# A state-space stage with its convolution, point-wise and input matrices folded on chip into three shifted matrices, and one slot per sequence

## The reference

```python
rms = sqrt(mean(T * T, axis=-1) + 1e-6)
Tn = T / rms * norm_scale                      # T: 16 x 256 x 256
x, z = split(Tn @ in_w.T + in_b, 2)            # in_w: 512 x 256
gate = sigmoid(z)
xc = conv1d(x, dw_w, padding=1, groups=256) + dw_b     # 3 taps, each feature by itself
xc = pw_w @ xc + pw_b                          # over the features
y = ssm(xc, forward) + flip(ssm(flip(xc), backward))
#   ssm: u = x @ win.T (64 states); h = h * Abar + u * Bbar, step by step; (h * C) @ wout.T
y = (y * gate) @ out_w.T + out_b
out = T + y
...
x = layernorm(x + out)                         # so 2 * x + y, normalized over the features
```

## Time and profile before

| | |
|---|---|
| median of three runs | 2217.35 us (2207.57, 2219.92, 2217.35) |
| profiled execution | 2220.97 us, its span 2219.1 us |
| busy in the span | PE 1861.8 (84%), DVE 1285.6 (58%), ACT 1025.6 (46%), POOL 338.1 (15%) |
| mean granted TensorE clock | 0.916 |

### The profile page before, as it was taken

The page is one execution under the profiler, slowest core; times in us unless marked ns, Lnnn a source line. Parts: engine busy times, 40 slices in busy tenths (PEclk is TensorE's granted clock), DMA queues, the critical chain, the costliest instruction groups (busy, mean ns, idle before and its releaser), DMA issues. The chain is left out here.

```text
span 2219.1 us, 39960 instructions
## 1 busy us (share of the span) xinstructions
PE 1861.8 (84%) x14981; PEld 1647.3 (74%) x15076; DVE 1285.6 (58%) x2769; ACT 1025.6 (46%) x2026; POOL 338.1 (15%) x522
## 2 busy tenths in 40 slices
PE   2799999859999994886467666885999999999998
PEld 1677777647878872554366656885999999999998
DVE  3566676536667664886477766882444443444453
ACT  1376776515555555554444424552333333343341
POOL 4443342011111102443000000000000000000000
PEclk9799999959999996998677878997999999999999
DMA  5876666168777736100000003212000000000000
GB/s 152 170 139 135 126 142 134 23 139 176 158 163 159 165 71 222 43 0 7 20 0 0 0 0 128 100 54 108 6 19 9 9 19 9 9 19 9 9 13 12
DMA packets 107698, 159.84 MB, mean 72 GB/s; under 512 B 13472, under 2 KB 86432, under 8 KB 103584
## 3 DMA queue, kind: packets, MB, share of 16 engines
q1 hardware_dynamic: 102464, 154.14, 28.7%
q10 hardware_dynamic: 5120, 4.20, 1.0%
HBM read 107.97 MB, written 49.81 MB: 71 GB/s over the span
## 5 line engine op out<-in xcount | busy, mean ns | idle before, releaser
L2035 ACT ACTIVATE ffn_slots<-ps,ffn_sh 128x256 f32<-128x256 f32 x256 | 107.5, 472 | 322.4 <-PE ps L1941 322.1
L1941 PE MATMUL ps<-ffn_uT_hi,h 128*128 128x256 f32 x1024 | 245.3, 283 | 2.4 <-DVE ffn_uT_lo L2095 2.4
L1941 PE MATMUL ps<-ffn_uT_lo,h 128*128 128x256 f32 x1024 | 245.1, 282 | 0.0
L1941 PE MATMUL ps<-ffn_gT_hi,ffn_h 128*128 128x256 f32 x1024 | 243.8, 281 | 0.0
L1941 PE MATMUL ps<-ffn_gT_lo,ffn_h 128*128 128x256 f32 x1024 | 243.7, 281 | 0.0
L1941 PEld LDWEIGHTS ps<-ffn_uT_hi,h 128*128 128x128 f32 x1024 | 193.9, 189 | 2.6 <-DVE ffn_uT_lo L2095 2.6
L1941 PEld LDWEIGHTS ps<-ffn_uT_lo,h 128*128 128x128 f32 x1024 | 193.9, 189 | 0.0
L1941 PEld LDWEIGHTS ps<-ffn_gT_hi,ffn_h 128*128 128x128 f32 x1024 | 192.8, 188 | 0.0
L1941 PEld LDWEIGHTS ps<-ffn_gT_lo,ffn_h 128*128 128x128 f32 x1024 | 192.7, 188 | 0.0
L218 POOL TENSOR_TENSOR shifted<-moments,eps 128x4 f32<-128x4 f32 (+1 forms) x32 | 11.8, 370 | 1042.2 <-DVE moments L189 1042.2
L679 ACT ACTIVATE cross_probs<-ps 128x512 f32<-128x512 f32 x192 | 115.3, 602 | 108.3 <-PE ps L489 70.3
(11 more groups left out here) (398 smaller groups left out, 5506.8 us busy)
## 6 DMA issues: line engine op xcount, KB each, us to landing
latent_split<-latent_qk_hi SPq DMA_DIRECT2D x16, 512.0 KB, 3.5
latent_split<-latent_qk_lo SPq DMA_DIRECT2D x16, 512.0 KB, 4.4
queries<-latent_split SPq DMA_DIRECT2D x32, 256.0 KB, 4.9
keys<-latent_split SPq DMA_DIRECT2D x32, 256.0 KB, 6.9
cross_split<-cross_qk_hi SPq DMA_DIRECT2D x16, 512.0 KB, 3.2
cross_split<-cross_qk_lo SPq DMA_DIRECT2D x16, 512.0 KB, 4.3
queries<-cross_split SPq DMA_DIRECT2D x32, 256.0 KB, 4.9
keys<-cross_split SPq DMA_DIRECT2D x32, 256.0 KB, 6.7
```

The lines of the kernel that those rows point to most:

```text
L1941: last = nc.tensor.matmul(out_ap, a, b, start=start and n == 0, stop=stop and n == 1, **kw)
L2035: last = nc.scalar.activation(slots[:, p % 2, a], halved(HIDDEN_BANK + p % 2)[:, a, :], ACT.Gelu, scale=scales[:, 2 * p + a:2 * p + a + 1])
```

## The change

**Loads.** The parameters of the stage are no longer loaded by it. The sync block of `quantized_feed_forward` issues 21 loads into tiles that live on to the state-space stage (`core.ssm_raw`), behind the loads of the feed-forward's own weights and before those of `core.to_stage`. The host hands pw_w and in_w's first half over in another orientation.

**Folding.** A block of its own, once per launch, multiplies matrices instead of data: mixed = pw_w times win (12 matmuls of 128 columns); `mixed_w[tap]` = mixed with its rows scaled by that tap's dw_w, in halves; in_w's first half times the three of them (12 matmuls of 384 columns), scaled by norm_scale: `taps_w`, three matrices from the normalized, transposed state straight to the input of the scans. A position's input is then the sum over three taps, each reading the transposed state shifted by a column in a tile with a zero column at each end. Sixteen float32 matmuls of a single column give what the biases come to: one sum for all positions, and for the first and last position the part of in_b that a tap outside the sequence must not bring (`edges`). The second half of in_w is scaled by norm_scale (`gate_w`) and wout by C.

**Per sequence** this leaves 18 matmuls for the three taps, 12 for the gate, 6 for the outputs, 12 for the projection. The convolution on VectorE, the padded copy, the products with pw_w and win and their halves are gone.

**Slots.** The loop is now written out on every engine: 22 slots from -4 to 17, in each of which an engine does the steps of several sequences, as `for s in SLOTS` shows. Tiles and PSUM banks alternate between even and odd sequences. The root and scaling of the state, two times the state plus out_b (`ssm_base`), the correction of the two end positions and mean, root and offset of the rows are on GpSimd; the final normalization is on ScalarE.

```diff
...
+                for dst, src in core.ssm_loads:
+                    sp.dma_start(dst, src).then_inc(core.ssm_in, 16)
                 for dst, src in core.to_stage:
                     sp.dma_start(dst, src).then_inc(core.weights_staged, 16)
...
-        split_weights(nc, core, "ssm_w", [(w["in_w"], *in_w), (w["pw_w"], *pw_w), (w["out_w"], *out_w)])
...
+                @block.tensor
+                def _(pe):
+                    pe.wait_ge(lo_done, 2)
+                    for m in range(DT):
+                        for c in range(DT):
+                            last = product(nc, ps[:, MIXED_BANK, m * P:(m + 1) * P], halves(pw_w, ALL, c, slice(m * P, (m + 1) * P)), halves(win, ALL, c), c == 0, c == DT - 1, skip_group_check=True)
+                    last.then_inc(mixed_raw, 1)
+                    pe.wait_ge(lo_done, 3)
+                    pe.wait_ge(mixed_ready, 1)
+                    for q in range(DT):
+                        for m in range(DT):
+                            last = product(nc, ps[:, FOLD_BANK + q, 0:TAPS * P], halves(inner_w, ALL, m, slice(q * P, (q + 1) * P)), halves(mixed_w, ALL, m), m == 0, m == DT - 1)
+                        last.then_inc(folded, 1)
+                    pe.wait_ge(mixed_copied, 1)
+                    for n, (left, right) in enumerate([(raw["win"][:, c, :], pw_b[:, c:c + 1]) for c in range(DT)] + [(mixed_f[:, m, :], dw_b[:, m:m + 1]) for m in range(DT)]):
+                        nc.tensor.matmul(ps[:, CONST_BANK, 0:1], left, right, start=n == 0, stop=n == 2 * DT - 1, skip_group_check=True)
+                    for tap in range(TAPS):
+                        for m in range(DT):
+                            for n in range(2):
+                                last = nc.tensor.matmul(ps[:, CONST_BANK, 1 + tap:2 + tap], f32(mixed_w[n][:, m, tap, :]), in_b[:, m:m + 1], start=m == 0 and n == 0, stop=m == DT - 1 and n == 1, skip_group_check=True)
+                    last.then_inc(constants_raw, 1)
+
...
+                    act.wait_ge(mixed_raw, 1)
+                    for m in range(DT):
+                        for tap in range(TAPS):
+                            last = nc.scalar.activation(mixed_w[0][:, m, tap, :], ps[:, MIXED_BANK, m * P:(m + 1) * P], ACT.Copy, scale=dw_w[:, m, tap:tap + 1])
+                    last.then_inc(mixed_hi, 1)
+                    nc.scalar.copy(mixed_f[:].rearrange("p c n -> p (c n)"), ps[:, MIXED_BANK, 0:DT * P]).then_inc(mixed_copied, 1)
...
+                    dve.wait_ge(mixed_hi, 1)
+                    dve.wait_ge(mixed_copied, 1)
+                    for m in range(DT):
+                        for tap in range(TAPS):
+                            last = nc.vector.scalar_tensor_tensor(mixed_w[1][:, m, tap, :], ps[:, MIXED_BANK, m * P:(m + 1) * P], dw_w[:, m, tap:tap + 1], f32(mixed_w[0][:, m, tap, :]), ALU.mult, ALU.subtract)
+                    last.then_inc(mixed_ready, 1)
...
+                    nc.vector.tensor_copy(constant_parts[:], ps[:, CONST_BANK, 0:1 + TAPS])
+                    dve.drain()
+                    nc.vector.tensor_reduce(bias[:], constant_parts[:], AX.X, ALU.add)
+                    nc.vector.tensor_scalar(edges[:], constant_parts[:, 1:1 + TAPS:TAPS - 1], drive[:], -1.0, ALU.mult, ALU.mult)
+                    dve.drain()
+                    nc.vector.tensor_mul(bias[:], bias[:], drive[:])
...
-            @block.sync
-            def _(sp):
-                for dst, src in loads:
-                    sp.dma_start(dst, src).then_inc(params_in, 16)
...
-                    for e in chains:
-                        pe.wait_ge(conv_ready, nth(j, e))
-                        for m in range(DT):
-                            for c in range(DT):
-                                last = product(nc, bank(e, PW)[:, m, :], halves(pw_w, slice(None), c, slice(m * P, (m + 1) * P)), halves(conv_p[e], slice(None), c), c == 0, c == DT - 1)
-                        last.then_inc(mix_raw, 1)
...
+                def inputs(i):
+                    pe.wait_ge(xT_ready, i + 1)
+                    if i >= 2:
+                        pe.wait_ge(u_driven, i - 1)
+                    for tap in range(TAPS):
                         for c in range(DT):
+                            last = product(nc, ps[:, U_BANK + i % 2, 0:S], halves(taps_w, ALL, c, tap), halves(xT[i % 2], ALL, c, slice(tap, tap + S)), tap == 0 and c == 0, tap == TAPS - 1 and c == DT - 1)
+                    last.then_inc(u_raw, 1)
...
+                def project(i):
+                    pe.wait_ge(gated_ready, i + 1)
+                    if i >= 1:
+                        pe.wait_ge(rows_added, i)
+                    for t in range(TT):
+                        for c in range(DT):
+                            last = product(nc, halved(O_BANK)[:, t, :], halves(gated_p[i % 2], ALL, c, slice(t * P, (t + 1) * P)), halves(out_w, ALL, c), c == 0, c == DT - 1)
+                    last.then_inc(out_raw, 1)
...
+                for s in SLOTS:
+                    if live(s + 2):
+                        inputs(s + 2)
+                    if live(s + 1):
+                        outputs(s + 1)
+                    if live(s + 3):
+                        turn_state(s + 3)
+                    if live(s + 2):
+                        gates(s + 2)
+                    if live(s):
+                        project(s)
...
+                def drive_states(i):
+                    act.wait_ge(u_raw, i + 1)
+                    if i >= 2:
+                        act.wait_ge(scanned, i - 1)
+                    nc.scalar.activation(driven[i % 2][:], ps[:, U_BANK + i % 2, 0:S], ACT.Identity, scale=drive[:], bias=bias[:]).then_inc(u_driven, 1)
...
+                for s in SLOTS:
+                    if live(s - 2):
+                        normalize(s - 2)
+                    if live(s + 4):
+                        square_state(s + 4)
+                    if live(s + 2):
+                        drive_states(s + 2)
+                    if live(s + 3):
+                        state_hi(s + 3)
+                    if live(s + 1):
+                        gated_high(s + 1)
+                    if live(s + 2):
+                        gate_inner(s + 2)
+                        states_hi(s + 2)
...
+                def double_state(i):
+                    if i >= 2:
+                        pool.wait_ge(rows_added, i - 1)
+                    nc.gpsimd.tensor_scalar(base[:, tiles(i)], state(i), 2.0, None, ALU.mult)
+                    pool.drain()
+                    nc.gpsimd.tensor_tensor(base[:, tiles(i)], base[:, tiles(i)], out_b[:].to_broadcast([P, TT, D]), ALU.add).then_inc(based, 1)
+
+                def correct_edges(i):
+                    pool.wait_ge(u_driven, i + 1)
+                    ends = driven[i % 2][:, 0:S:S - 1]
+                    nc.gpsimd.tensor_tensor(ends, ends, edges[:], ALU.add).then_inc(driven_ready, 1)
...
+                def normalize_state(i):
+                    pool.wait_ge(squared, i + 1)
+                    nc.gpsimd.tensor_tensor(ms[:, tiles(i)], square_sum[:, tiles(i)], ms_eps[:, tiles(i)], ALU.add)
+                    pool.drain()
+                    nc.gpsimd.tensor_tensor(inv_rms[:, tiles(i)], ms[:, tiles(i)], core.minus_half[:, tiles(i)], ALU.pow).then_inc(rms_ready, 1)
+                    pool.drain()
+                    if i >= 2:
+                        pool.wait_ge(xT_raw, i - 1)
+                    for n in range(TT * (i % 2), TT * (i % 2 + 1)):
+                        last = nc.gpsimd.tensor_scalar(normed[:, n, :], tile_of(core, i, n % TT), inv_rms[:, n:n + 1], D ** 0.5, ALU.mult, ALU.mult)
...
-                def convolve(e, j):
-                    dve.wait_ge(x_padded, nth(j, e))
-                    for c in range(DT):
-                        nc.vector.tensor_scalar(conv[e][:, c], padded[e][:, c, 0:S], dw_w[:, c, 0:1], dw_b[:, c:c + 1], ALU.mult, ALU.add)
-                    for tap in (1, 2):
-                        dve.drain()
-                        for c in range(DT):
-                            last = nc.vector.scalar_tensor_tensor(conv[e][:, c], padded[e][:, c, tap:tap + S], dw_w[:, c, tap:tap + 1], conv[e][:, c], ALU.mult, ALU.add)
...
+                def add_rows(i):
+                    dve.wait_ge(out_raw, i + 1)
+                    dve.wait_ge(based, i + 1)
+                    if i >= 2:
+                        dve.wait_ge(normalized, i - 1)
+                    nc.vector.tensor_add(core.rows[:, tiles(i)], halved(O_BANK), base[:, tiles(i)]).then_inc(rows_added, 1)
...
+                def scan_states(i):
+                    dve.wait_ge(driven_ready, i + 1)
+                    if i >= 2:
+                        dve.wait_ge(y_hi, i - 1)
+                    for n, order in enumerate((slice(None), slice(None, None, -1))):
```

(32 more changed lines are left out.)

443 lines of the change are left out of this document (202 added, 241 removed).

## The result

The changed kernel takes 2090.09 us (median of four, 2083.56 to 2092.28) against 2218.64 for the kernel before; the ratio is 0.943, with a 95% interval of 0.9394 to 0.9466. The forecast was 2086 with 2066 to 2112. The profiled execution took 2090.99 us, its span 2089.2.

The account below looks back on a forecast made before the run. Chains bound the state-space stage; after the change GpSimd's 7.3 us slot would. Start, 18 slots, dips and end sum to 150.7 us against 282.95, 132 less, giving 2086 us, range 2066 to 2112.

Parts of the forecast that it names:

- What bounds before: State-space stage before the change, 282.95 us: no engine full, held by chains of handovers in which paired sequences move in step.
- Loads and folding: Start of the stage: early parameter loads cost nothing, entry 0.9 us, folding block 19 (16 to 22), change of block 0.3.
- The slot: Full slot of the stage's loop: 7.3 us, GpSimd's own work 5.9 plus 1.4 lost; range 6.9 to 7.8, chance 0.53.
- doubling 128x512: GpSimd's doubling of the state in each slot, priced at 0.69 us from rows of 256 and 1024 columns.
- The friction: SBUF port shared by VectorE and GpSimd: two-input VectorE instructions hold GpSimd up, 1.41 us lost a slot.
- the root isn't in the way: GpSimd's root within a slot: runs beside two-input VectorE instructions without loss, 1.01 us in an earlier trace.
- TensorE at 6.0: TensorE's own work in a slot, 48 products and four transposes with restarts: 6.0 us, the slot without friction.
- The sum: Whole state-space stage: start, 11 full slots at 7.3 us, seven light ones for 35.3, dips and end; 150.7 us.
- Strict lock, or GpSimd slower than its rows: slot 8.4: Rival for the slot: the root too holds scans back, or GpSimd is slower; 8.4 us, time 2106, chance 0.2.
- TensorE as the bound: Rival for the slot: GpSimd's losses fall where it would wait anyway; 6.0 us, time 2069, chance 0.17.
- half clock: Rival for the slot: TensorE's clock stays at half; 11.0 us, time 2148, chance 0.07.
- the ring: Rival for the slots: waits make four engines work one after another; 22.7 us a slot, time 2325, chance 0.03.

Follow-up runs that it names:

- half-bias kernel: Changed kernel without GpSimd's doubling: GpSimd adds half of out_b to the state, VectorE's addition doubles the sum; 2064.79 us, ratio 0.9334.

## Why the prediction was right

The time was forecast at 2086 us and is 2090.09. That the stage is held by chains, that the folding and the slots shorten them and that GpSimd with its lost time then sets the slot is what the runs show. The length of the slot was wrong. By it the 18 slots took 9.6 us more than forecast and the stage, whose start was shorter, 8.0 more; 5.6 of these were made up for by the other stages in the profiled execution.

- **What bounds before** held: chains. The folding takes the wait for the convolved tile out. That for the low half of the states stays as long as sequences go in pairs (17.2 us in six pairs of the run without the slots), and the slots nearly remove it (0.4 us in all from 1072 to 1195).
- **Loads and folding.** 18.1 us from the stage's start to the first square, where entry, folding and the change of block were put at 20.2. The first products of 384 columns started 9.3 us in, the one-column products took 3.8 (3.3 to 6.7 were given, by the clock). The forecast costed the early loads at nothing; no run shows a cost, and without them the stage is 13.8 us longer.
- **From squares to taps** 5.8 for 5.2.
- **The slot: the step that failed.** The forecast was 7.3 us and the slot is 8.36, outside the 6.9 to 7.8 of its case. The term that was mis-sized is "doubling 128x512, between 0.48 for 256 and 1.12 for 1024 columns, 0.69": it takes 1.50. Both rows are of tensor_scalar with two operations (times a scale, plus a rounding constant, in the feed-forward's code), the doubling has one, and no row showed a wide one with one. With two operations the same kernel has 7.48. So of the 1.06 us that the slot is longer, 0.81 are the doubling's, 0.09 the friction's, and some 0.15 are left in GpSimd's other terms.
- **The friction** was right in kind and sum: 0.41 + 0.40 + 0.51 + 0.18 = 1.50 us lost (0.61, 1.09, 0.71 and 0.38 against 0.20, 0.69, 0.20 and 0.20), for 1.41. Its layout was wrong in one place: "the root isn't in the way" was read from the earlier trace rows, where the root starts 0.2 us before the instructions with two inputs. Started inside the scan, it waits like the others; with the decay in PSUM it doesn't.
- **TensorE at 6.0** as the floor: 6.14, shown once GpSimd was relieved. The shifted taps cost nothing: in those slots their products start 0.118 us apart (median), as those with wout do.
- **The sum.** Of the eleven full slots of the forecast ten were full, and one had 7.15. Ten at 8.36 for 7.3 are 10.6 us more; 18 slots took from 1071.55 to 1201.74, where the last addition starts, 130.2 for 120.6. The stage has 158.7 for 150.7. The other stages were 5.6 us shorter in this execution than in the one before, by which the forecast of a profiled 2088.7 and the measured 2090.99 came close. So the time is nearer to the forecast than its working deserves, and that is luck. The forecast also called itself wrong if another stage changed by over 3 us. The three stages ahead together are 3.2 us shorter, but by the spread given above a single pair of executions can't show such a change.
- **The rivals.** "Strict lock, or GpSimd slower than its rows: slot 8.4" has the slot that was measured. Its second half is what happened. Its first half isn't: with a strict lock a root that runs would hold a scan back, and the last rows of this document show one that doesn't. Its 2106 was too high by the light slots and the dips, which it made longer too (they stayed near 6.0, and the clock at 0.92), and by the shorter start and the other stages. TensorE as the bound came one experiment later, half clock and the ring not at all.

## What to carry to other kernels

When work is moved to the engine with the most room, add up that engine's own slot, and take each price from a row of the same instruction form, not only of the same name and width; a form that no row shows is measured alone first. Where VectorE and GpSimd work side by side, list VectorE's instructions with two SBUF inputs and see what of GpSimd's starts inside them: one operand put into PSUM, or one instruction moved, may free more than it seems. And once the fullest engine is relieved, the next bound is near: here 8.36 went to 6.14 at one edit, and there TensorE has no gap left.

## What the runs showed of the hardware

- On GpSimd, tensor_scalar over 512 float32 columns takes 1.50 us with one operation and 0.62 with two (1.57 with one from a tile; 0.84 and 0.52 over 256).
- The Trainium skill's "SBUF — State Buffer", section "Who interferes with whom", calls the port pair that VectorE and GpSimd share an exclusive lock, and says that whoever issues first gets it for the whole instruction. It says the latter of VectorE's two-port modes; the prediction took it for two SBUF inputs as well. Where VectorE is first the traces agree (0.61, 0.71 and 0.38 above). Where GpSimd is first it depends on the instruction. Each pair below is from an early slot, and the low half of the states, 0.42 alone, starts inside a wide GpSimd instruction. With the addition of 512 columns (half-bias kernel) and with the doubling in two operations it ends some 0.3 us behind that instruction, as the lock would have it:

```profile
1081.90 1.63 POOL L1590 TENSOR_TENSOR ssm_base<-state,ssm_raw_out_b 128x512 f32<-128x512 f32 x1
1082.30 1.51 DVE L1671 TENSOR_TENSOR ssm_y_lo<-ssm_states,ssm_y_hi 128x256 fp32r<-128x256 f32 x1
...
1086.78 0.96 POOL L1589 TENSOR_SCALAR ssm_base<-state 128x512 f32<-128x512 f32 x1
1087.17 0.83 DVE L1672 TENSOR_TENSOR ssm_y_lo<-ssm_states,ssm_y_hi 128x256 fp32r<-128x256 f32 x1
```

With the doubling in one operation (changed kernel) it doesn't:

```profile
1084.69 0.68 DVE L1668 TENSOR_TENSOR ssm_gated_p_lo<-ssm_gated,ssm_gated_p_hi 128x512 fp32r<-128x512 f32 x1
...
1084.90 1.84 POOL L1589 TENSOR_SCALAR ssm_base<-state 128x512 f32<-128x512 f32 x1
1085.29 0.83 DVE L1672 TENSOR_TENSOR ssm_y_lo<-ssm_states,ssm_y_hi 128x256 fp32r<-128x256 f32 x1
```

The doubling starts inside the first low half and gets 0.34 us longer, as the one with two operations does (0.96 for 0.62). The second low half has 0.83 us in either case. But here it ends at 1086.12, 0.62 before the doubling's end at 1086.74. So the 0.88 us by which the form with one operation is longer don't shut VectorE out. GpSimd's spans are rough in the profile, so how long each of its instructions holds VectorE is told by VectorE's own 1.51 and 0.83.

- The root, 0.70 us on GpSimd, doesn't hold a scan that starts while it runs. The two scans have 1.37 us here, no more than elsewhere (1.38; changed kernel):

```profile
1082.42 0.70 POOL L1611 TENSOR_TENSOR ssm_inv_rms<-ssm_ms,minus_half 128x2 f32<-128x2 f32 x1
1082.68 1.37 DVE L1659 TENSOR_TENSOR_SCAN ssm_states<-ssm_decay,ssm_driven 64x256 f32<-64x256 f32 x2
```
